# Decoder block on one core: self-attention scores sixteen pairs ahead, maxima transposed six slots ahead, row loads spread out

## The reference

```
x = x + self_attention(layernorm(x))       # 32 heads of 32, 8 key/value heads, q/k/v/o weights are signs times row scales
x = x + cross_attention(layernorm(x), ctx) # 16 heads, low-rank query and key/value projections
x = x + feed_forward(layernorm(x))         # low rank 256, inner 2752, silu(gate) * up
```

## Time and profile before

| | us |
|---|---|
| median of 3 runs | 1601.66 |
| lowest, highest | 1598.12, 1612.58 |
| the profiled execution | 1598.57 |
| its span, first to last instruction | 1596.8 |
| busy in it: PE, DVE, ACT, POOL | 1409.5, 936.7, 707.6, 483.1 |

### The profile page before, as it was taken

How to read it: one execution, slowest core, us unless ns; L and a number is a source line. 1 busy time by engine, 2 the same in 40 slices (tenths; PEclk the granted TensorE clock), 3 DMA queues, 4 the chain that set the end, 5 groups by cost and what they waited for, 6 DMA issues and landing times.

```text
span 1596.8 us, 22580 instructions
## 1 busy us (share of the span) xinstructions
PE 1409.5 (88%) x8423; PEld 989.6 (62%) x8423; DVE 936.7 (59%) x1643; ACT 707.6 (44%) x1584; POOL 483.1 (30%) x434
## 2 busy tenths in 40 slices
PE   5877899789978998687888989887899999999998
PEld 3545455545554555345766767675788888888886
DVE  5477555755565456454857758466374573673645
ACT  5164603441344124402765747475454444453442
POOL 2045402551254225611212112113252242252331
PEclk9998999899988998988999999998899999999999
DMA  5865454626451644136554636345610220220111
GB/s 185 115 117 128 94 84 97 114 41 114 99 108 29 113 107 61 41 139 178 145 146 106 176 90 171 93 106 155 234 55 1 78 81 1 79 80 0 67 66 53
DMA packets 94880, 157.54 MB, mean 99 GB/s; under 512 B 9910, under 2 KB 49076, under 8 KB 94772
## 3 DMA queue, kind: packets, MB, share of 16 engines
q1 hardware_dynamic: 94772, 156.11, 39.2%
HBM read 82.15 MB, written 25.17 MB: 67 GB/s over the span
## 4 chain that ended last, share of the span: by engine, by line
PE 67%; DVE 12%; DMA 8%; ACT 5%; issue 4%; SPq 3%; POOL 1%; DVEq 0%; ACTq 0%; POOLq 0%
PE bank L935 15%; PE bank L947 7%; PE bank L861 7%; PE bank L742 6%; PE bank L776 4%; DMA q_stack<-top_rows 3%; PE bank L920 3%; PE bank L696 3%; PE bank L756 3%; PE bank L875 3%; PE bank L789 2%; PE bank L819 2%; PE bank L960 2%; PE bank L846 2%; PE bank L802 2%
## 5 line engine op out<-in xcount | busy, mean ns | idle before, releaser
L1465 POOL TENSOR_TENSOR fold<-wide 128x512 f32<-128x512 f32 x128 | 163.0, 1274 | 321.0 <-ACT wide L1015 235.7
L1268 DVE TENSOR_REDUCE neg_top<-bank 128x2 f32<-128x512 f32 x256 | 171.3, 684 | 88.3 <-PE bank L756 87.6
L1015 ACT ACTIVATE wide<-bank 128x512 f32<-128x512 f32 x256 | 150.8, 596 | 146.7 <-PE bank L776 142.7
L776 PE MATMUL bank<-q_stack,k_stack 98*128 98x512 f32 x256 | 144.5, 567 | 61.3 <-DMA q_stack<-top_rows 59.9
L1537 POOL TENSOR_TENSOR v_lo<-v_all,v_hi 128x512 fp32r<-128x512 f32 x88 | 122.7, 1396 | 247.4 <-ACT v_hi L1100 247.4
L935 PE MATMUL bank<-pT_hi,v_hi 128*128 128x512 f32 x352 | 137.3, 390 | 2.6 <-POOL v_lo L1537 2.6
L935 PE MATMUL bank<-pT_hi,v_lo 128*128 128x512 f32 x352 | 137.1, 390 | 0.0
L935 PE MATMUL bank<-pT_lo,v_hi 128*128 128x512 f32 x352 | 137.0, 389 | 0.0
L1422 DVE SCALAR_TENSOR_TENSOR inner<-bank,b_cols,inner 128x512 f32<-128x512 f32 x88 | 66.0, 750 | 112.6 <-PE bank L935 109.3
L1032 ACT ACTIVATE wide<-bank,neg_max 128x256 f32<-128x256 f32 x256 | 120.0, 489 | 8.3 <-DVE neg_max L1298 8.3
L776 PEld LDWEIGHTS bank<-q_stack,k_stack 98*128 98x128 f32 x256 | 51.4, 202 | 106.5 <-DMA q_stack<-top_rows 71.2
(11 more groups left out here) (176 smaller groups left out, 3106.5 us busy)
## 6 DMA issues: line engine op xcount, KB each, us to landing
q_stack<-hi_lo SPq DMA_DIRECT2D x96, 256.0 KB, 5.6
xin<-x_scratch SPq DMA_DIRECT2D x33, 512.0 KB, 4.5
xq_stack<-xhi_lo SPq DMA_DIRECT2D x128, 128.0 KB, 2.4
x_res<-in_x SPq DMA_DIRECT2D x19, 512.0 KB, 4.6
x_scratch<-x_res SPq DMA_DIRECT2D x16, 512.0 KB, 2.7
xin<-in_ctx SPq DMA_DIRECT2D x16, 512.0 KB, 4.6
x_group<-x_scratch SPq DMA_DIRECT2D x32, 256.0 KB, 3.5
x_scratch<-x_group SPq DMA_DIRECT2D x32, 256.0 KB, 2.6
```

The costliest lines, as they stand in the source:

```text
L776: pe.matmul(tiles[m % 2][:, :], kst[0:SUB + 2, tq, b * SEQ + kt * P:b * SEQ + (kt + 1) * P], qst[U % Q_STACKS][0:SUB + 2, 2 * hp:2 * hp + ...
L1015: act.activation(PT[m % PT_RING][:, :], tiles[m % 2][:, :], ACT.Exp).then_inc(sem["tile_exped"], 1)
L1268: dve.tensor_reduce(neg_top[U % 2][:, r, b, :], tops[n % 2][:, :].rearrange("p (a b) -> p a b", a=QT), AX.X, ALU.max, negate=True).then_in ...
L1465: pool.tensor_tensor(fold[f % FOLD_RING][:, :], PT[2 * f % PT_RING][:, :], PT[(2 * f + 1) % PT_RING][:, :], ALU.add).then_inc(sem["folded" ...
```

## The change

`LEAD` goes from 12 to 16 pairs. `top` moves from slot 5 of the unit ahead to slot 1, and ahead of the side work. The query tiles 4 to 7 of a group are placed two slots later. The next group's row loads, with their norms five slots behind each, stand at slots 7, 15, 23 and 31 (15, 20, 24 and 31 in group 0) instead of 24, 25, 26 and 33, and the fourth uses the ring `x_res`. Its turns move from slots 32 to 39 to slots 34 to 41, and its first three query tiles from slots 40 to 63 to slots 43 to 63. Between groups all sixteen first scores go with the output projection, two to each half tile. In group 0 the query tile 2 carries a score with each chunk instead of with every second.

```diff
-LEAD = UH + 4
+LEAD = 2 * UH
...
-        order += part + ([score(0, UH + c // 2)] if c % 2 else [])
+        order += part + [score(0, UH + c)]
...
-                put((tq - 4) * UH + c, *part)
+                put((tq - 4) * UH + 2 + c, *part)
...
-            for m in range(3):
-                put(24 + m, ("load", "x", g + 1, m))
-                put(28 + m, ("norm", "x", g + 1, m))
-            put(33, ("load", "x", g + 1, 3))
-            put(36, ("norm", "x", g + 1, 3))
+            for m, at in enumerate((7, 15, 23, 31) if g else (15, 20, 24, 31)):
+                put(at, ("load", "x", g + 1, m))
+                put(at + 5, ("norm", "x", g + 1, m))
             for m in range(TILES):
                 for h in range(2):
-                    put(32 + 2 * m + h, *turn("x", g + 1, m, h))
-            for tq in range(3):
-                for c, part in enumerate(q_parts(g + 1, tq)):
-                    put(40 + tq * UH + c, *part)
+                    put(34 + 2 * m + h, *turn("x", g + 1, m, h))
+            chunks = [part for tq in range(3) for part in q_parts(g + 1, tq)]
+            for c, part in enumerate(chunks):
+                put(43 + c * 21 // len(chunks), *part)
...
+            if i % UH == 1 and i // UH + 1 < KV_HEADS:
+                step += top(g * KV_HEADS + i // UH + 1)
             step += side.get(i, [])
...
-            if i % UH == 5 and i // UH + 1 < KV_HEADS:
-                step += top(g * KV_HEADS + i // UH + 1)
...
-            for c in range(4):
+            for c in range(UH):
                 order += [score(n, 2 * c), score(n, 2 * c + 1)] + stream[c]
                 if c == 3:
-                    order.append(("o_load", g, 2))
-            order += top(n * KV_HEADS)
-            for c in range(2):
-                order += [score(n, UH + 2 * c), score(n, UH + 2 * c + 1)] + stream[4 + c]
-            order += stream[6] + stream[7] + [("o_load", g, 3)]
+                    order += top(n * KV_HEADS) + [("o_load", g, 2)]
+            order.append(("o_load", g, 3))
...
-            ring = "xres" if (ph, g) == ("x", 0) and m != 2 or (ph, g, m) == ("z", 0, 3) else "xin"
+            ring = "xres" if (ph == "x" and (m == 3 or g == 0 and m != 2)) or (ph, g, m) == ("z", 0, 3) else "xin"
```

## The result

The changed kernel takes 1562.13 us in the median of 4 runs (1553.73 to 1564.34), the kernel before 1606.56 (4 runs, 1598.12 to 1612.58): a ratio of 0.9725, 95% interval 0.9697 to 0.9753. It is 44 us faster. The profiled execution took 1561.65 us (span 1559.9), 36.9 less than the one of before, against the 65.5 of the sum.

A forecast was written before the change was run, and what follows sets the result against it. Bound: TensorE in the self-attention head loops, with 59.9 us of waits for row maxima and a lowered clock. Terms -60 + 5 + 2.5 + 4 + 3 - 20 = -65.5 gave 1533, median 1535; own range 1518 to 1552, 8-in-10 1516 to 1566.

The forecast's parts named there:

- rival (2): Head loops: VectorE's maximum or the query stack takes back 30 us of the removed wait; 1563 us, chance 0.13.
- 0 to 12, I take +4: VectorE's queue: statistics ahead of finish delay scores 0.5 to 1 us in some 8 plain units; +4 us.
- Maxima, -60: Head loops: transposing the row maxima in slot 1, ahead of finish, removes TensorE's 59.9 us wait for the rows.
- This is what lets the transpose move.: Claim that issuing scores sixteen pairs ahead is what allows the maxima's transpose to go to slot 1.
- Query stack and start: Less room for the query stack, 16 times, +5 us (0 to 16); first score's wait at the start, +2.5 (1 to 5).
- Rival (4): Query stack becomes the bound in 16 places, 4.9 us each, and the kernel gets slower; 1626 us, chance 0.02.
- Nothing of its own: Query tiles two slots later on SyncE: the tile they wait for is done by slot 9; no cost or gain.
- Is through before the next unit's rows: Row loads, one per unit: each follows 768 KB of stack and finishes before the next unit's row DMAs.
- Turns, +3: Units with turns: only the row waits go, and small waits on VectorE take some of their place; +3 us.
- Clock, -20: Head loops: of 82 us at the lower clock, half of a possible 41 us comes back; -20 us (0 to -41).
- rival (1): Row waits go but the clock doesn't recover, small waits holding it down; 1555 us, chance 0.11.
- The signs: Expected loop times, clock of 0.95 or more, unchanged stretches between groups, and score waits over 20 us as refutation.

The follow-up runs named there:

- scale_later: Changed kernel with GpSimd's layer-norm scaling of groups 1 to 3 as its own step, one slot behind the statistics; 1550.78 us, ratio 0.9674.
- norm_early: Changed kernel with layer-norm statistics and scaling of groups 1 to 3 at slot 2 instead of slot 4; 1547.88 us, ratio 0.9651.
- top_slot5: Changed kernel with the maxima's transpose back at slot 5, behind side work and finish; 1622.11 us, ratio 1.0108.
- top_first: Kernel before, with the transpose moved within slot 5 ahead of side work and finish, nothing else; 1558.57 us, ratio 0.9724.
- lead12: Changed kernel with statistics at slot 2, scores 12 pairs ahead, transpose in slot 5 directly behind the score; 1544.56 us, ratio 0.9623.
- both: Changed kernel, still 16 ahead, with statistics at slot 2, GpSimd's scaling three slots behind, group 0's first scores in slots 4 to 7; 1544.03 us, ratio 0.9626.
- query_old: Changed kernel with query tiles 4 to 7 of a group back in their old slots, two earlier; 1575.40 us, ratio 0.9823.
- loads_only: Kernel before with only the spread row loads, their statistics five slots behind, and the fourth load's other ring; 1615.15 us, ratio 1.0066.
- combo: Changed kernel with statistics at slot 2 and group 0's first eight loop scores two by two in slots 4 to 7; 1549.07 us, ratio 0.9660.

## Why the prediction was right in sign and its gain half as large again as measured

The forecast was 1535, the median 1562: inside the 8-in-10 range and above the forecast's own, which ends at 1552. It lies near rival (2), that "the wait changes its name". The name is right, VectorE's maximum and the query stack, which together grew by 30.6 us. That its 1563 is met so closely is luck: it had some 15 us less idle time (-45.5 + 30) and 20 less for the clock, and the runs show 34.5 and 7.7. Of the 28.6 us missing in the profiled execution, 11 are idle time (34.5 us went, 45.5 forecast), 12.3 are busy time, where the clock shows (7.7 against 20), and 5.3 lie behind the self-attention. The prediction's "own range" has a slip: 1533 less 21 for the clock is 1512, not 1518, and so its lower end lies below the 1516 of the wider range. Nothing else rests on it.

**The step that failed: "0 to 12, I take +4" for VectorE's queue.** The list's entry grew by 21.8 us (0.6 to 22.4). The mechanism was right, statistics in slot 4 ahead of finish in slot 5; the size of each wait and the number of places were not. I put 0.5 to 1 us on "some 8 units of plain length". Six of those waited 1.8 us each, 10.8 in all: inside the range of the term and nearly three times its value. That is longer than the 0.5 to 1 us, because the product was costed at its length beside an idle GpSimd: in scale_later it is 0.4 us shorter and the wait too, so without the whole 0.8 us of stretch some 1.0 us would be left, an estimate. The trace of the kernel before has the longer one already, in a unit with statistics; VectorE, then GpSimd:

```profile
307.11 1.54 DVE L1294 TENSOR_TENSOR attnT<-attnT_raw,recip_rows 128x512 f32<-128x512 f32 x1
```

```profile
306.91 1.19 POOL L1475 TENSOR_SCALAR xin<-xin,bn 128x1024 f32<-128x1024 f32 x1
```

The 0.8 us of stretch were GpSimd's fold pushed late by its own share of the same norm, which the prediction didn't move through GpSimd's queue. scale_later and norm_early show this part. Of the other seven waits one is 0.15 us. Three, of 1.5 to 2.0 us and 4.9 in all, are in group 0 ahead of the turns and had no term. Three, of 2.18 us and 6.5 in all, are in the units with turns, where the prediction had small waits on VectorE "take some of their place" for +3.

**Maxima, -60.** Right: the entry is gone. That the transpose's place ahead of finish carries the gain is shown from both sides, by top_slot5 (the gain goes) and top_first (it comes alone).

**"This is what lets the transpose move."** True of slot 1 (with 12 pairs ahead, the eighth score of the next unit is issued in slot 3), but the gain does not need slot 1. top_first moves the transpose past finish with 12 pairs ahead, and lead12 is as fast as both (they differ in the lead, the transpose's slot, the scaling and the start). Sixteen ahead buys room that is not needed, and pays with stack waits and the start.

**Query stack and start.** Forecast +5 and +2.5. The stack entry grew by 8.8 us over the span, 4.56 of it the wait at the start, forecast as "some 4.4". The other 4.2 are mostly three waits in group 3, of 1.0, 0.4 and 2.2 us, where "some 0 to 1 us ones" had been named at four slots. The part ahead of the first tile grew 2.9 with the four scores that it took in. Rival (4) would have needed 2.8 us in 16 places.

**"Nothing of its own" for the query tiles.** Wrong: 13 to 16 us, by query_old. I looked at what the stack's blocked entry holds up among the row DMAs, and not at the row load that stands in that same slot.

**Row loads.** "Is through before the next unit's rows" was right for the changed kernel. By themselves they are a loss of 10 us, shown by loads_only. The change needs the new query slots with them.

**Turns, +3.** The waits on VectorE there came to 6.5 us, as said; they are part of the 21.8. TensorE's other waits fell by some 5 us.

**Clock, -20.** Mis-sized. The time at the lower level in the four loops fell from 82 us to 45. But the stretches ahead of, between and behind them gained some 7, so that the self-attention fell from 96 us to 65, by 31. TensorE was busy in 79 of those 96 us and in 55 of the 65. So 24 us of work at the lower level went, and 6 of idle time, which no clock shortens. Half of the 24 would be the 12 that busy time should have lost, and it fell by 7.7. The term of 20 was half of what the 82 us would give back with TensorE full; the 31 that went gave back 7.7. Why the 24 gave a third and not a half is open; between other pairs of these kernels (norm_early and the changed one, top_slot5 and the one before) it was nearly half. The page "TensorE: Matmul & The Clock Gate" of the Trainium skill (Terms), weighed in the prediction, would give 15 us for the 31, an estimate; the trace has 7.7.

Against rival (1) the prediction said that units without a long wait are at clock 1.00, from one plain unit. The same trace falls to the lower level at 502.2, at 601.1 and at 642.1 us, at the end of or right behind waits of 2.3, 1.7 and 2.6 us for the rows. Behind the wait of 1.7 us (clock 0.51), in the columns of the earlier trace rows:

```profile
601.10:604.00 2.90, 2.90 (x9) 1.89 (x10) 0.89 (x2) 1.19 (x2) 0.96 (x1) 0.51 1.03 165
```

**The signs.** Loops of 109, 108, 110 and 91 us, where 107, 106, 109 and 91 were named; the wait at the start came as named; the clock in the loops was 0.92 to 0.98, where "0.95 or more" was. The stretches between groups were to stay as they are, and grew by 1.1 to 1.6 us each with the scores that they took in. The forecast had named a total of over 20 us of waits of the score matmul as a sign against it: there were 33.5.

## What to carry to other kernels

Before a step is costed as moved, follow it through every engine's queue: here the wait that the change was made for (the rows' subtraction behind finish) and the two surprises (fold behind the scaling, load behind the blocked stack) are all one instruction standing in an in-order queue behind a neighbour that it doesn't need. Try the smallest reordering first: one step moved within its slot gave all that the whole change gave, and only then could it be seen what the rest was worth. And where an elementwise product has two SBUF inputs, take its duration from rows with GpSimd busy beside it.

## What the hardware showed that was not expected

A VectorE product with two SBUF inputs that runs beside a GpSimd operation ends 0.53 to 0.56 us behind that operation's end (1.45 and 1.04 us instead of 0.69, with the fold and the scaling), and in the other order, with the product first, the scaling takes 1.53 instead of 1.20. Maxima and transposes in the same stretches keep their 0.69 and 0.71.

The same idle time can go with very different clocks: top_slot5 and the kernel before are idle for 109.4 and 110.4 us, and TensorE is busy 20.6 us longer in the first, for the same work, with 136 us at the lower level against 96. The other way round, norm_early and scale_later cut 4.8 and 3.3 us of idle time, and busy time fell by 7.2 and 6.4. That the clock ties the two is read from the profiles, one execution each; what sets it is not settled here.

Still open: what the clock's share of busy time follows from, why combo's start, 4.56 us of wait shorter, gives 0.8 us, and what the waits of group 0 cost by themselves. No run took VectorE's sign work out of that group.
